# Second mixers: both token halves' parameter rows in one PSUM bank, one 32x512 split, parameter matmuls in other slots, cross block dropped

## The reference, cut to what matters

```python
def _mamba(x, Win, convw, convb, Wx, Wdt, bdt, Alog, Dp, Wout):   # x: [2, 2048, 256]
    xi, z = jnp.split(x @ Win, 2, axis=-1)                         # 512 + 512 channels
    xi = silu(causal_dwconv(xi, convw, convb))                     # 4 taps
    xdbc = xi @ Wx                                                 # 16 dt rows, 16 B rows, 16 C rows
    dt = softplus(xdbc[..., :16] @ Wdt + bdt)
    h = scan(exp(dt * A) * h + (dt * xi) * B)                      # 16 states per channel
    y = sum over the 16 states of h * C, + xi * Dp
    return (y * silu(z)) @ Wout
```

## Time and profile before

| | us |
|---|---|
| median of 3 runs | 3488.31 (3487.5 to 3493.22) |
| profiled execution | 3491.77 |
| span of its trace | 3490.0 |
| VectorE busy in the span | 2849.4 (82%) |
| TensorE busy | 2785.7 (80%) |
| GpSimd busy | 2257.3 (65%) |
| ScalarE busy | 1801.3 (52%) |
| granted TensorE clock, mean | 0.92 |

### The profile page before, as it was taken

How to read it: one execution, slowest core, us unless ns; L and a number is a source line. 1 busy time by engine, 2 the same in 40 slices (tenths; PEclk the granted TensorE clock), 3 DMA queues, 4 the chain that set the end, 5 groups by cost and what they waited for, 6 DMA issues and landing times. The chain is left out here.

```text
span 3490.0 us, 25014 instructions
## 1 busy us (share of the span) xinstructions
PE 2785.7 (80%) x7718; PEld 1176.7 (34%) x7718; DVE 2849.4 (82%) x2290; ACT 1801.3 (52%) x2391; POOL 2257.3 (65%) x1098
## 2 busy tenths in 40 slices
PE   6677767665568888888788798798798897779899
PEld 2223222453223333333333333233233332234344
DVE  6999899542369999999999999999999999678300
ACT  5775776231355665555655555555555654333211
POOL 3696498001239889899889899798898898401000
PEclk7899799878778999999999999999999899989899
DMA  1011011237424555454554555454545545321000
GB/s 64 30 48 36 26 49 49 79 143 282 149 86 171 168 174 174 170 175 166 173 188 163 170 181 181 164 175 172 172 169 176 175 157 205 120 88 49 12 18 24
DMA packets 164789, 451.46 MB, mean 129 GB/s; under 512 B 23472, under 2 KB 52336, under 8 KB 164624
## 3 DMA queue, kind: packets, MB, share of 16 engines
q1 hardware_dynamic: 158896, 428.89, 36.0%
q0 software_dynamic: 5760, 20.97, 1.5%
HBM read 414.94 MB, written 34.87 MB: 129 GB/s over the span
## 5 line engine op out<-in xcount | busy, mean ns | idle before, releaser
L1385 POOL TENSOR_TENSOR mix_prod<-mix_spread,mix_h 128x1024 f32<-128x1024 f32 x512 | 1368.0, 2674 | 238.2 <-DVE mix_h L1791 121.8
L1885 PE MATMUL mix_banks<-mix_prod,kept_ident 128*128 128x512 f32 x2048 | 1048.3, 638 | 90.0 <-POOL mix_prod L1385 63.3
L1435 ACT ACTIVATE mix_side_in<-mix_dt,mix_neg_a 128x1024 f32<-128x1024 f32 x384 | 437.6, 1141 | 304.4 <-DVE mix_h L1791 300.9
L1885 PEld LDWEIGHTS mix_banks<-mix_prod,kept_ident 128*128 128x128 f32 x2048 | 403.0, 202 | 527.7 <-issue 303.0
L1777 DVE TENSOR_TENSOR mix_banks<-mix_banks,mix_dtu 128x1024 f32<-128x1024 f32 x384 | 467.3, 1217 | 6.1 <-POOL mix_dtu L1375 3.8
L1791 DVE TENSOR_TENSOR_SCAN mix_h<-mix_side_in,mix_state,mix_banks 128x1024 f32<-128x1024 f32 x192 | 450.6, 2347 | 17.4
L1791 DVE TENSOR_TENSOR_SCAN mix_h<-mix_side_in,mix_banks 128x1024 f32<-128x1024 f32 x192 | 439.0, 2286 | 18.8 <-ACT mix_side_in L1435 1.3
L1875 PE MATMUL mix_banks<-mix_parts,kept_sel 96*128 96x512 bf16 x768 | 247.3, 406 | 246.0 <-DVE mix_h L1791 237.9
L410 POOL TENSOR_TENSOR mix_drive<-mix_drive,mix_du 128x1024 f32<-128x1024 f32 x128 | 304.8, 2396 | 150.7 <-ACT mix_drive L481 150.7
L1395 POOL TENSOR_TENSOR mix_side_in<-mix_spread,mix_dtu 128x512 f32<-128x512 f32 x256 | 332.5, 1299 | 0.1
L633 DVE TENSOR_TENSOR_SCAN mix_h<-mix_banks,mix_state,mix_drive 128x1024 f32<-128x1024 f32 x128 | 296.1, 2339 | 14.2 <-POOL mix_drive L410 9.3
(11 more groups left out here) (264 smaller groups left out, 4297.1 us busy)
## 6 DMA issues: line engine op xcount, KB each, us to landing
mix_spread<-c_rows SPq DMA_DIRECT2D x640, 512.0 KB, 3.8
mix_c_row<-c_rows SPq DMA_DIRECT2D x40, 512.0 KB, 3.6
exa_f<-f SPq DMA_DIRECT2D x32, 512.0 KB, 7.0
slot_outputs<-exa_inter POOLq DMA_DIRECT2D x32, 512.0 KB, 7.4
ln_zp<-slot_outputs SPq DMA_DIRECT2D x8, 2048.0 KB, 7.8
first_acc<-xT SPq DMA_DIRECT2D x8, 512.0 KB, 7.5
x_scratch<-first_acc POOLq DMA_DIRECT2D x8, 512.0 KB, 3.2
fw_scratch<-mix_res SPq DMA_DIRECT2D x8, 512.0 KB, 7.0
```

The costliest lines, as they stand in the source:

```text
L1385: pool.tensor_tensor(prod[:, un % 2, :], spread[:, i % SLOTS, :], h[:, un % HR, :], ALU.mult).then_inc(prod_ready, 1)
L1435: act.activation(drive[un % 2] if pooled(un) else side_in[:, un % 2, :], dt[:, at // NS, :], ACT.Exp, scale=neg_a[:, way(p), at:at + 1]).t ...
L1885: mm = pe.matmul(y_bank[:, hf, :], k.ident[:], half(prod[:, un % 2, :], hf), start=False, stop=True, skip_group_check=True)
```

## The change

Both halves' rows now go into one bank: partitions 0 to 15 hold the B rows of half 0, 16 to 31 those of half 1, then likewise C (32 to 63) and dt (64 to 95). The stationary side is a window of 96 columns into a zero-padded `wx` of 112 columns, shifted by 16 for the other half; all 16 matmuls accumulate into one bank. The second B copy is gone, the DRAM tensor is `par_rows` with one row of 512 tokens per kind, half and state, and a row load fetches two such rows. `spread_b` uses a second selector (`sel_late`) for half 1, `step_rows` a `wdt` of two zero-padded blocks. `keep_par`, `rest_of` and the split run once per pass on 32x512; `keep_par` moves to slot 52, `rest_of` to 53, `less_mid` to 55, `par` to slots 47, 49, 50, 51. `project` adds x by one matmul with the identity; the tile `centre` is gone. `sq` and the split's scratch lie in a tile that was there already.

```diff
-def selectors(pool, k, built):
-    pool.memset(k.sel[:], 0.0).then_inc(built, 1)
+def selectors(pool, sel, built, row=0):
+    pool.memset(sel[:], 0.0).then_inc(built, 1)
     for part in range(3):
         pool.wait_ge(built, 1 + part)
-        pool.affine_select(out=k.sel[:], in_=k.sel[:], compare_op=ALU.not_equal, fill=1.0, base=-32 * part,
+        pool.affine_select(out=sel[:], in_=sel[:], compare_op=ALU.not_equal, fill=1.0, base=-32 * part - row,
                            pattern=[[-1, NS], [0, P]], channel_multiplier=1).then_inc(built, 1)
...
-                order += [(47, 0, ("par", p + 1, 0)), (48, 0, ("par", p + 1, 1))]
+                order.append((47, 0, ("par", p + 1)))
...
-    c_rows = nc.dram_tensor("c_rows", (NP * 2 * NS, TC), F32, kind="Internal").ap()
+    par_rows = nc.dram_tensor("par_rows", (NP, 2, 2, NS, TT), F32, kind="Internal").ap()
...
-        wx, wdt = m.sb("wx", [P, MB, 64 + R]), m.sb("wdt", [64 + R, D2])
+        wx, wdt = m.sb("wx", [P, MB, 112]), m.sb("wdt", [96, 2, D2])
...
-                return ((wx[:, :, 64:64 + R], src[:, :, 0:R]), (wx[:, :, 0:NS], src[:, :, R:R + NS]),
-                        (wx[:, :, 32:32 + NS], src[:, :, R + NS:R + 2 * NS]),
-                        (wx[:, :, 32 + NS:32 + 2 * NS], src[:, :, R:R + NS]))
+                return ((wx[:, :, 80:80 + R], src[:, :, 0:R]), (wx[:, :, 16:16 + NS], src[:, :, R:R + NS]),
+                        (wx[:, :, 48:48 + NS], src[:, :, R + NS:R + 2 * NS]))
+            def w_dt(way):
+                src = a[("fw", "bw")[way] + "_Wdt"]
+                return (wdt[64:64 + R, 0, :], src), (wdt[64 + R:96, 1, :], src)
...
                 if p + 1 < NP and s == 53:
-                    sp.wait_ge(c_kept, 2 * (p + 1) + 2)
-                    sp.dma_start(c_rows[(p + 1) * 2 * NS:(p + 2) * 2 * NS, :], c_row).then_inc(c_stored, 16)
+                    sp.wait_ge(c_kept, p + 2)
+                    sp.dma_start(par_rows[p + 1].rearrange("k h n t -> (k h n) t"), rows[0:64, :]).then_inc(c_stored, 16)
                     sp.wait_ge(c_stored, 16 * (p + 2))
...
-                row = un // UNITS * 2 * NS + un % NS + (0 if kind == "c" else NS)
-                sp.dma_start(spread[:, i % SLOTS, :], c_rows[row:row + 1, :].broadcast_to((P, TC))
+                n = un % NS
+                row = par_rows[un // UNITS, 1 if kind == "c" else 0, :, n:n + 1, :].rearrange("h o t -> o h t")
+                sp.dma_start(spread[:, i % SLOTS, :].rearrange("p (h t) -> p h t", h=2), row.broadcast_to((P, 2, TT))
                              ).then_inc(row_loaded[i % SLOTS], 16)
...
+            selectors(pool, sel_late, sel_built, NS)
...
-                act.activation(half(dtin, hf), bank[64:64 + R, :], ACT.Copy)
-                act.activation(half(c_row, hf), bank[32:32 + 2 * NS, :], ACT.Copy).then_inc(c_kept, 1)
-                if p >= 2 and hf == 0:
+                act.activation(rows[:], bank[0:96, :], ACT.Copy).then_inc(c_kept, 1)
+                if p >= 2:
                     act.wait_ge(b_spread, by_dve(unit_no(p - 1, 0, 0)))
-                act.activation(half(parts[0:32, p % 2, :], hf), bank[0:32, :], ACT.Copy).then_inc(high, 1)
+                act.activation(parts[0:32, p % 2, :], bank[0:32, :], ACT.Copy).then_inc(high, 1)
...
-                    if s == 50:
-                        keep_par(p + 1, 0)
-                    if s == 51:
-                        keep_par(p + 1, 1)
+                    if s == 52:
+                        keep_par(p + 1)
...
-                dve.tensor_tensor(half(rest, hf), side_bank(*key)[0:32, :], half(parts[0:32, p % 2, :], hf),
+                dve.tensor_tensor(rest, side_bank(*key)[0:32, :], parts[0:32, p % 2, :],
                                   ALU.subtract).then_inc(free[steps.bank(*key)], 1)
...
-                    if s == 51:
-                        rest_of(p + 1, 0)
-                    if s == 52:
-                        rest_of(p + 1, 1)
-                    if s == 54:
+                    if s == 53:
+                        rest_of(p + 1)
+                    if s == 55:
                         less_mid(p + 1)
...
-            dve.memset(wx[:], 0.0).then_inc(cleared, 1)
+            dve.memset(wx[:], 0.0)
+            dve.memset(wdt[64:96, :, :], 0.0).then_inc(cleared, 1)
...
-            dve.tensor_scalar(centre[:, 0, :], k.ident[:], 1.0, -1.0 / E, ALU.mult, ALU.add)
-            dve.memset(centre[:, 1, :], -1.0 / E)
...
                 for g in (2 * pair, 2 * pair + 1):
-                    mm = pe.matmul(bank[0:64 + R, :], wx[:, g, :], half(u[:, p % 2, g, :], hf), start=g == 0, stop=g == MB - 1)
+                    mm = pe.matmul(bank[0:96, :], wx[:, g, 0:96] if hf else wx[:, g, 16:112], half(u[:, p % 2, g, :], hf),
+                                   start=first and g == 0, stop=last and g == MB - 1)
...
-                    mm = pe.matmul(bank, wdt[64:64 + R, g * P:(g + 1) * P], half(dtin, hf), start=True, stop=True)
+                    mm = pe.matmul(bank, wdt[64:96, hf, g * P:(g + 1) * P], rows[64:96, :], start=True, stop=True)
...
-                    for c1 in range(C):
-                        mm = pe.matmul(bank, centre[:, 0 if c == c1 else 1, :], xs(p, c1, hf), start=False, stop=c1 == C - 1)
+                    mm = pe.matmul(bank, k.ident[:], xs(p, c, hf), start=False, stop=True)
...
-                    mm = pe.matmul(half(drive[un % 2], hf), k.sel[:, at % NS, :], half(parts[:, p % 2, :], hf),
+                    mm = pe.matmul(half(drive[un % 2], hf), (sel_late if hf else k.sel)[:, at % NS, :], parts[:, p % 2, :],
...
-                    if 47 <= s < 51:
-                        par(p + 1, (s - 47) % 2, (s - 47) // 2)
+                    for n, s0 in enumerate((47, 49, 50, 51)):
+                        if s == s0:
+                            par(p + 1, n % 2, n // 2)
```

More of the change, by code:

```diff
@@ L1329, in side @@
                     sp.wait_ge(full[steps.bank("xi", p, MB - 1, 1)], steps.full("xi", p, MB - 1, 1))
-                    sp.wait_ge(full[steps.bank("par", p, 1)], steps.full("par", p, 1))
+                    sp.wait_ge(full[steps.bank("par", p)], steps.full("par", p))
                     for dst, src in (w_in(1, 0), *w_x(1)):
@@ L1334, in side @@
                     sp.wait_ge(full[steps.bank("dt", p, 3, 1)], steps.full("dt", p, 3, 1))
[L1335 removed]
+                    for dst, src in w_dt(1):
+                        sp.dma_start(dst, src).then_inc(wdt_loaded, 16)
                 if p == WAY - 1 and s == 62:
```

51 lines of the change are left out of this document (26 added, 25 removed).

## The result

The changed kernel is slower: 3501.61 us median (3496.12 to 3507.69, 6 runs) beside 3487.9 us (3482.28 to 3496.05, 6 runs) for the kernel before, a ratio of 1.0033 with a 95% interval of 1.0016 to 1.0049. The forecast was 3467.9, in a range up to 3479. The profiled execution took 3500.81 us, of which the span is 3499.0.

The account below looks back on a forecast made before the run. VectorE was taken to bound the kernel, at work 246.2 of 253 us in a middle pass. Terms 4.1 + 2.1 + 1.4 + 9.0 + 3.4 + 1.5 - 1.1 = 20.4 us took 3488.31 to 3467.9; range 3460 to 3479.

Parts of the forecast that it names:

- part 4: SP's queue: store delays row loads, GpSimd's 1.6 us wait covered; two-piece row loads 0.8 us later, hidden; cost 0.
- Rival C: Row loads cost the DMA engines time per piece, not per byte, making them the bound: 3516 us, chance 0.05.
- rival B: Row wait behind the store reaches VectorE, 1.6 us in each of 7 passes: 3479 us, chance 0.10.
- Part 1: VectorE's split, 7 passes: one subtraction fewer 4.1 us, its waiting gone 2.1, the 32x1024 subtraction made 32x512 1.4.
- rival D: VectorE's 32x512 difference beside GpSimd work takes its worst time in each pass: 3474 us, chance 0.08.
- Part 2: TensorE's parameter matmuls leave slot 48, so slot 50's gate wait in five passes nearly goes: 9.0 us gained.
- Rival A: Slot 50's gate wait stays, with TensorE's low clock as argument, all else stands: 3476.9 us, chance 0.15.
- Parts 3 and 4 (the store): ScalarE's fewer copies give nothing inside passes; the later store's 1.6 us GpSimd wait in 7 passes is covered, cost 0.
- Rival E: Nothing gained inside passes, VectorE's savings return as waits for GpSimd's products, only the ends count: 3484.5 us, chance 0.06.
- Part 5: Cross block: one fp32 matmul fewer per output half, 0 in the passes, 3.4 us behind the last scan.
- Part 6: Ramp before the first unit gains 1.5 us; larger clearing at the start costs 1.1 us.

Follow-up runs that it names:

- e4: Changed kernel, each partition loading two 2 KB pieces of its own from an input, 2 MB apart, in place of the shared row: 3457.84 us, one run.
- e3: Changed kernel with the two 2 KB pieces of a row 2.5 KB apart and four stores: 3465.18 us, ratio 0.9927.
- e5: Changed kernel with one unused 2 KB row behind each block of 16 (halves 34 KB apart) and four stores: 3467.0 us, ratio 0.9927.
- g2: e5 with one store of 64 rows in place of four: 3469.21 us, ratio 0.9941.
- e2: Kernel before with only its rows stored as halves 64 KB apart and loaded in two 2 KB pieces: 3505.27 us, ratio 1.0047.
- e1: Changed kernel with the two halves of a row side by side, loaded as one 4 KB piece, and four stores: 3467.68 us, ratio 0.9935.
- e6: e1 with the parameter matmul pairs back in slots 47 to 50: 3469.86 us, ratio 0.9944.
- e9: e5 with the 32x512 difference back in slot 54 instead of 55: 3465.32 us, ratio 0.9938.
- f1: Kernel before with only the parameter matmuls moved to slots 47, 49, 50, 51, second half's copies and subtraction one slot later: 3478.9 us, ratio 0.9976.
- e7: e1 with the cross block restored, two fp32 matmuls per output half: 3467.17 us, ratio 0.993.
- e11: Like e5, but with the two pieces of a row 32 KB and 512 bytes apart: 3480.49 us, one run.
- e12: Like e5, but both pieces of a row load are the same 2 KB, the first half read twice: 3475.73 us, one run.

## Why the prediction was wrong

**The step that failed** is the second half of part 4, "Cost 0" for the 640 row loads in two pieces of 2 KB. I took their landing time from mix_lin (4.6 us) and their rate from the 2 KB loads of the earlier trace rows, and called the first "of that very shape". It has the shape on the side of SBUF; in memory its partitions each read an address of their own. A row load sends 128 partitions to the same 2 KB, twice. e4 measures the case that I had priced, 3.8 us and cheap; the real one is 5.8. That the row is shared is not enough for the loss: at 2.5, 4 and 34 KB between the pieces it lands in 4.2 to 4.3 us. What was dear is the shared row with its halves 32 KB apart. So "a row is asked for about three units before its product, so 0.8 us more is hidden" was applied to an extra of 0.8 us where the extra was 2.0 in the median (the longest landing went from 9.1 to 12.2), and GpSimd's lead did not hide that: its waits for rows went from 3.7 us to 34.5. The first half of part 4 was off too: the store was to hold SP's queue for 3.1 us, and held it for up to 6.5. The prediction's own signs of being wrong, a share well above 0.51 and waits of VectorE for a spread, are what the trace then showed.

**Rival C** had the sign and the place, and a time (3516) that is nearer than the forecast; its mechanism fell with e3 and e5. Nor did the DMA engines become the bound: their share stayed at 0.65. The cost is the landing time of single rows (and of the store among them), which reaches VectorE through GpSimd's order and TensorE's, most of all behind the store of slot 53. There rival B's mechanism came in: its cover of three units holds when a row lands in 4.2 us (g2, 1.4 us of GpSimd waiting for rows in all) and not when it lands in 5.8. The size of this: e5 against the changed kernel is 34.6 us in the medians, e2 against the kernel before 17. Of the 31.6 us between the passes of e5 and of the changed kernel, 10.6 are VectorE's instructions running longer (1951.2 for 1940.6 us busy) and 21.0 idle time, 13.9 of that spent waiting for spreads. In e2, half of the 9.9 us in front of the gates went while the rows came late (4.8 left): the kernel before had waits that late rows could share. That this is all of the difference between 17 and 34 isn't shown.

**The rest of the sum held as a whole, to a few us**, by e5, where only the rows are repaired. Segments of its profiled execution, to be set beside the table above: 61.21, 1990.23 and 45.77 us, so 1.4, 15.7 and 3.3 us less than before, 20.4 in all, which is the forecast's sum to the tenth. The exact match is luck, since kernels whose rows are all cheap differ by 14 us in their passes (e3 1982.64, e5 1990.23, e1 1991.37, g2 1996.44), and by g2's trace the sum would be 14.1. By medians the repaired kernels stand 17 to 24 us below the kernel before, at 3467 to 3469 (e1, e5, g2).
- Part 1: the split. 7 subtractions of 0.653 us remain of the 14 of the earlier trace rows, 4.6 us for 9.3, and nothing waits in front of them: right. The 32x512 difference was to give 1.4 us and gave none, a mean of 1.320 us beside 1.290. The shortest and longest show why, line L1664 of the changed kernel (ns shortest, median, longest):
```profile
L1664 DVE TENSOR_TENSOR mix_x<-mix_x x8: 652/668/2544, 990.1 to 2743.4; 32x512 f32<-32x512 f32 x8
```
  Of the seven in the passes four take 0.65 us, as assumed for one alone; the other three take 1.98 to 2.54. So rival D, the worst each time, did not come in either. The longest starts at 2743.41, 0.35 us after a product of GpSimd (at 2743.06, which takes at least 2.3 us), and ends at 2745.95. I took the mean excess of L1667; the measured one was 0.67 us. The Trainium skill (SBUF — State Buffer, Who interferes with whom) has the two shut each other out for a whole instruction; the longest, 2.544 us, agrees with it. In e6 and e9 the step takes 0.81 us in the mean and 1.01 at most.
- Part 2: right in size when it stands alone (f1), and the gate waits went in every kernel with the new slots. Rival A did not come in. The low clock is there as before, behind 3.61 us without work (granted 0.72 from 1438 to 1444 in pass 1), but sum 47 behind it takes 1.88 us, and the gates wait 0.9 us in all. On top of the other parts it seems worth less (e6).
- Parts 3 and 4 (the store): no wait that VectorE shows while the rows are cheap. In g2 GpSimd waits 1.4 us for rows in all, where I had allowed 1.6 in each of 7 passes. Rival E, by which only the 3.8 us of the ends would be left, fell with the same kernels, 17 to 24 us below the kernel before.
- Part 5: 3.4 forecast, 3.65 in the traces of e1 and e7; too small for the medians.
- Part 6: 0.4 us net forecast, 1.2 to 1.4 measured from the clearing to the softplus step. The clearing of the changed kernel itself took more than I gave it:
```profile
936.75 0.43 DVE L1759 MEMSET mix_wx<- 128x448 f32 x1 [5.04 <-PEq L53]
937.43 0.91 DVE L1760 MEMSET mix_wdt<- 32x1024 f32 x1 [0.25 <-issue]
```
  From 936.75 to 938.34 is 1.6 us for the old 0.325, so 1.3 for my 1.1. So the ramp behind it gained some 2.6 us, where the forecast had 1.5.

What stays open: how addresses map to the memory behind it, why e11 is fast with late rows, and how the gain of some 20 us divides among the parts, since the passes of like kernels differ by more than single terms of a few us, and the terms seem not to add. Of the kernels that compute all of the reference, e1, e3, e5, e6 to e9, f1 and g2 beat both the kernel before and the changed one; g2 is the changed kernel with one unused row per block and nothing else.

## What to carry to other kernels

Price a load that all partitions take from one row by another such load, with its pieces placed alike: here a load of the same shape on the SBUF side, whose partitions read their own addresses, did not give its time. Keep such a row in one piece, or try an unused row between its parts, and read the landing time of the issues before and after. An edit that takes a wait from the bounding engine can shift it against its neighbours, so measure such edits together as well as alone.

## What the runs showed of the hardware that I had not expected

- 2 KB pieces of a shared row land in 4.2 to 4.3 us at 2.5, 4 and 34 KB from each other (4.0 in one piece, e1) and 1.6 to 2.2 us later at 8, 16, 32 and 64 KB (5.8 to 6.4); 512 bytes added to 32 KB do not help (5.7), 2 KB do. The run at 64 KB is the kernel before with split rows; those at 8 and 16 KB and with the 512 bytes are one each.
- At 512 KB the same load is dear in the first three passes (share 0.63 to 0.69) and cheap in the others (0.52 to 0.56).
- Reading the same 2 KB twice per partition takes 5.3 us (e12, one run) for 4.0 with the whole row in one piece, at equal bytes.
- The Trainium skill (DMA: Bandwidth & Descriptors, Latency and other measured facts) reports that copies slow down when the rows of neighbouring partitions lie a large power of two apart, little at 512 KiB and by half at 4 MiB, cured at 4 MiB by 4 KiB of padding and not by 192 bytes. That is a distance from partition to partition; here it lies between two pieces of a row that all partitions share. These runs agree in kind (2 KB cure it, 512 bytes don't), but show it from 8 KB on, where e4's pieces 2 MB apart, a pair of its own for each partition, landed in 3.8 us.
